# An FFN's transposed 32x32 squares by way of DRAM in place of SBUF-to-SBUF transfers

## The reference

```python
def _L0_ffn_ref(x, W1, b1, quantum_phases, quantum_weights_real, quantum_weights_imag, W2, b2):
    def _quantum_transform(hidden, theta, w_real, w_imag):
        imag = w_imag * jnp.sin(theta + hidden * 0.1)
        quantum_phase = jnp.cos(theta) * w_real + jnp.sin(theta) * w_imag
        return hidden + quantum_phase * imag * 0.1
    hidden = jnp.einsum('bsd,df->bsf', x, W1) + b1
    q = _quantum_transform(hidden, quantum_phases, quantum_weights_real, quantum_weights_imag)
    act = jax.nn.relu(q)
    return jnp.einsum('bsf,fd->bsd', act, W2) + b2
x = x + _L0_xattn_ref(_layernorm(x, axis=-1), ctx_768, ...)
x = x + _L0_ffn_ref(_layernorm(x, axis=-1), ...)
```

## Time and profile before

| | us |
|---|---|
| median of 3 runs | 2107.33 (2104.51 to 2107.42) |
| profiled execution | 2109.2 |
| its span, first to last instruction | 2107.4 |
| TensorE busy in the span | 2060.1 (98%) |
| VectorE, ScalarE, GpSimd busy | 1350.2, 1146.9, 1047.2 |
| mean granted TensorE clock | 0.995 |

### The profile page before, as it was taken

One profiled execution on the slowest core, in us unless ns is written; L12 is line 12 of the kernel. 1 busy time (PEld: TensorE's weight loads), 2 busy tenths in 40 slices (PEclk: granted clock), 3 DMA queues, 4 the chain that ended last, 5 costly groups with the idle time before them and its releaser, 6 DMA issues.

```text
span 2107.4 us, 27424 instructions
## 1 busy us (share of the span) xinstructions
PE 2060.1 (98%) x9746; PEld 1716.9 (81%) x9746; DVE 1350.2 (64%) x2024; ACT 1146.9 (54%) x2036; POOL 1047.2 (50%) x757
## 2 busy tenths in 40 slices
PE   7999999999999979999999999999999999999999
PEld 5888888888887868888888888888888888887877
DVE  5888898888876746555465554655556555465554
ACT  4766667667664645444554545545455444554543
POOL 3777777777775434353343533435334353343521
PEclk9999999999999989999999999999999999999999
DMA  5122232232213311101011010110101101011000
GB/s 180 56 93 93 81 101 97 84 101 80 75 56 121 99 31 44 58 17 44 21 43 58 17 44 21 42 59 17 44 20 43 58 18 44 21 44 58 14 27 20
DMA packets 123386, 118.25 MB, mean 56 GB/s; under 512 B 73961, under 2 KB 74473, under 8 KB 123249
## 3 DMA queue, kind: packets, MB, share of 16 engines
q1 hardware_dynamic: 122096, 115.93, 17.3%
q10 hardware_dynamic: 1152, 0.56, 0.1%
HBM read 66.10 MB, written 34.62 MB: 48 GB/s over the span
## 4 chain that ended last, share of the span: by engine, by line
PE 65%; SPq 13%; DVE 9%; ACT 4%; issue 4%; DMA 4%; POOL 1%; DVEq 0%; POOLq 0%; ACTq 0%
PE psum L1091 21%; PE psum L1093 20%; PE psum L1092 20%; SPq L431 13%; DMA xn<-stage 3%; PE psum L1172 2%; DVE hid L1024 2%; DVE xt_lo L1057 2%; PE psum L1097 1%; ACT act_hi L779 1%; DVE stage L1082 1%; DVE stage L1078 1%; DVE act_lo L1027 1%; ACT hid L790 1%; ACT frac L775 1%
## 5 line engine op out<-in xcount | busy, mean ns | idle before, releaser
L612 POOL TENSOR_TENSOR frac<-turns,frac 128x512 f32<-128x512 f32 x256 | 339.6, 1326 | 846.3 <-DVE frac L1052 846.3
L1091 PE MATMUL psum<-w_hi,act_hi 128*128 128x512 f32 x1024 | 401.6, 392 | 15.9 <-DVE act_lo L1027 15.9
L1024 DVE SCALAR_TENSOR_TENSOR hid<-frac,gain,hid 128x512 f32<-128x512 f32 x256 | 315.2, 1231 | 133.5 <-ACT frac L775 132.4
L1093 PE MATMUL psum<-w_hi,act_lo 128*128 128x512 f32 x1024 | 399.5, 390 | 0.0
L1092 PE MATMUL psum<-w_lo,act_hi 128*128 128x512 f32 x1024 | 399.4, 390 | 0.0
L779 ACT ACTIVATE act_hi<-hid 128x512 fp32r<-128x512 f32 x256 | 161.8, 632 | 366.1 <-DVE hid L1024 366.1
L788 ACT ACTIVATE turns<-psum,u_shift 128x512 f32<-128x512 f32 x256 | 176.5, 689 | 308.8 <-PE psum L1093 235.2
L1027 DVE SCALAR_TENSOR_TENSOR act_lo<-hid,act_hi 128x512 fp32r<-128x512 f32 x256 | 201.4, 787 | 178.8 <-ACT act_hi L779 178.8
L1052 DVE TENSOR_SCALAR frac<-turns 128x512 f32<-128x512 f32 x256 | 111.6, 436 | 221.5 <-ACT turns L788 221.4
L1091 PEld LDWEIGHTS psum<-w_hi,act_hi 128*128 128x128 f32 x1024 | 192.9, 188 | 63.5 <-DVE act_lo L1027 12.8
L1093 PEld LDWEIGHTS psum<-w_hi,act_lo 128*128 128x128 f32 x1024 | 192.8, 188 | 40.2
(11 more groups left out here) (147 smaller groups left out, 4179.4 us busy)
## 6 DMA issues: line engine op xcount, KB each, us to landing
res<-in_x SPq DMA_DIRECT2D x64, 256.0 KB, 2.9
x_dram<-res SPq DMA_DIRECT2D x64, 256.0 KB, 2.0
x_sb<-x_dram SPq DMA_DIRECT2D x16, 1024.0 KB, 5.5
x_sb<-in_x SPq DMA_DIRECT2D x15, 1024.0 KB, 5.9
xn<-stage SPq DMA_DIRECT2D x480, 32.0 KB, 1.9
out<-x_sb SPq DMA_DIRECT2D x15, 1024.0 KB, 4.5
stage<-in_w SPq DMA_DIRECT2D x32, 256.0 KB, 2.8
v_in<-v_dram SPq DMA_DIRECT2D x16, 128.0 KB, 3.0
```

The source lines that it names most:

```text
L612: pool.tensor_tensor(frac[:, j % 2, :], turns[:, j % 2, :], frac[:, j % 2, :], ALU.subtract)\
L1024: dve.scalar_tensor_tensor(out=hid[:, j % 2, :], in0=frac[:, j % 2, :], scalar=gain[:, f:f + 1], in1=hid[:, j % 2, :], op0=ALU.mult, op1=A ...
L1091: pe.matmul(o, a_hi, b_hi, start=first, stop=False)
L1093: return pe.matmul(o, a_lo, b_hi, start=False, stop=last)
```

## The change

The turned squares take another way. Per half SyncE writes `stage` to a DRAM buffer `turn_dram` in 4 transfers, one for each group a of 32 partitions, 4 KB a partition in four runs of 1 KB (128 KB a transfer), and later reads the half back into `xn` in one transfer of 128 partitions, 4 KB of contiguous DRAM a partition, put down in sixteen runs of 256 B (512 KB). A new semaphore pair `moved` counts the writes. VectorE's transposes wait for `moved`, where they waited for `turned_in`; ScalarE's copy waits for the reads. SyncE issues both halves' writes first, then waits for `moved[0]` and issues the first read, then the same for the second. Before the writes of a later tile it waits for the former reads (`turned_in`). The squares' order in `stage` and `xn` changes with it (`turned`, `channels`): VectorE's transposes write and ScalarE's and VectorE's copies read at other strides.

```diff
-TURNS = NB * NB
...
-        turn_done, turned_in = sem("turn_done"), sems("turned_in", 2)
+        turn_done, moved, turned_in = sem("turn_done"), sems("moved", 2), sems("turned_in", 2)
...
-        to_turn = xn[:].rearrange("p n c -> p (n c)").rearrange("p (q h x) -> p h q x", h=2, q=KC * NB)
-        turned = stage[:].rearrange("p s c -> p (s c)").rearrange("p (q x) -> p q x", q=KC * NB)
-        squares_out = stage[:].rearrange("p s c -> p (s c)").rearrange("p (k b x) -> p k b x", k=KC, b=NB)
-        squares_in = xn[:].rearrange("p n c -> p (n c)").rearrange("p (k a h x) -> p h k a x", k=KC, a=NB, h=2)
-        channels = xn[:].rearrange("p n c -> p (n c)").rearrange("p (k a n i) -> p k n a i", k=KC, a=NB, i=SQ)
+        to_turn = xn[:].rearrange("p n c -> p (n c)").rearrange("p (k b h x) -> p h k b x", k=KC, b=NB, h=2)
+        turned = stage[:].rearrange("p s c -> p (s c)").rearrange("p (b k x) -> p k b x", b=NB, k=KC)
+        squares_out = stage[:].rearrange("p s c -> p (s c)").rearrange("p (b y) -> p b y", b=NB)
+        squares_in = xn[:].rearrange("p n c -> p (n c)").rearrange("p (q h x) -> p h q x", q=KC * NB, h=2)
+        moved_out = turn_dram.rearrange("h b j a y -> h a j b y")
+        moved_in = turn_dram.rearrange("h b j a y -> h (b j) (a y)").rearrange("h p (q x) -> h p q x", q=KC * NB)
+        channels = xn[:].rearrange("p n c -> p (n c)").rearrange("p (a k n i) -> p k n a i", k=KC, a=NB, i=SQ)
...
                 for half in range(2):
                     sp.wait_ge(turn_done, 2 * t + half + 1)
+                    if t:
+                        sp.wait_ge(turned_in[half], 16 * t)
                     for a in range(NB):
-                        for b in range(NB):
-                            sp.dma_start(squares_in[b * SQ:(b + 1) * SQ, half, :, a, :],
-                                         squares_out[a * SQ:(a + 1) * SQ, :, b, :]).then_inc(turned_in[half], 16)
+                        sp.dma_start(moved_out[half, a], squares_out[a * SQ:(a + 1) * SQ]).then_inc(moved[half], 16)
+                for half in range(2):
+                    sp.wait_ge(moved[half], 16 * NB * (t + 1))
+                    sp.dma_start(squares_in[:, half], moved_in[half]).then_inc(turned_in[half], 16)
                 sp.wait_ge(y2_done, NB * (t + 1))
...
                     for half in range(2):
-                        act.wait_ge(turned_in[half], 16 * TURNS * (t + 1))
+                        act.wait_ge(turned_in[half], 16 * (t + 1))
...
                     if t:
-                        dve.wait_ge(turned_in[1], 16 * TURNS * t)
+                        dve.wait_ge(moved[1], 16 * NB * t)
...
                     dve.wait_ge(xn_done, TILES + t + 2)
-                    dve.wait_ge(turned_in[0], 16 * TURNS * (t + 1))
+                    dve.wait_ge(moved[0], 16 * NB * (t + 1))
...
+    turn_dram = nc.dram_tensor("turn_dram", (2, NB, P // NB, NB, 2 * C // NB), F32, kind="Internal").ap()
```

More of the change, by code:

```diff
@@ L112, in xattn_ffn @@
 def xattn_ffn(nc, x, ctx_768, wq, bq, wk, bk, wv, bv, wo, bo, w1, b1, phases, w_real, w_imag, w2, b2,
-              out, x1_dram, v_dram, u_dram):
+              out, x1_dram, v_dram, u_dram, turn_dram):
     x_rows = x.rearrange("b (t n p) c -> (b t) p n c", n=NB, p=P)
@@ L1351 @@
     u_dram = nc.dram_tensor("u_dram", (B, C), F32, kind="Internal").ap()
-    xattn_ffn(nc, *args, out, x1_dram, v_dram, u_dram)
+    turn_dram = nc.dram_tensor("turn_dram", (2, NB, P // NB, NB, 2 * C // NB), F32, kind="Internal").ap()
+    xattn_ffn(nc, *args, out, x1_dram, v_dram, u_dram, turn_dram)
     r = run_bass_kernel_spmd(nc, [arrays], core_ids=[0])
```

## The result

| | before | after |
|---|---|---|
| median, us | 2107.38 (4 runs, 2104.51 to 2109.45) | 2084.03 (4 runs, 2082.80 to 2084.35) |
| ratio | | 0.9889, 95% interval 0.9872 to 0.9906 |
| span of the profiled execution | 2107.4 | 2082.6 |
| TensorE busy | 2060.1 | 2051.2 |
| granted clock | 0.995 | 0.998 |

The change makes the kernel 1.1% faster; 2083.5 us had been forecast. In the changed file the lines are 5 further down: L1083 and L1087 are the transposes, L801 the copy to xt_hi, L1062 the one to xt_lo, L1032 act_lo; L434 is now a write, L437 a read.

The account below looks back on a forecast made before the run. TensorE's holes in the tile turns, from chains of 2 x 16 issues at 0.64 us, were taken as what can be won: 13.8 (turns) + 10.0 (tile 0) = 23.8 us off 2107.33 gives 2083.5 us; range 2079 to 2100, about 8 in 10.

Parts of the forecast that it names:

- What bounds: TensorE is busy 2060.1 of 2107.4 us; only its holes, in the turns between FFN tiles, can be won.
- Issues: SyncE, per half: 16 issues become 4 at 0.64 us; the fourth write goes out after 1.9 us, lands in 1.93 us.
- signs of being wrong: A half's pieces over 4.3 us, a read's issue holding SyncE for microseconds, or DRAM writes landing later than 2 us.
- Second transpose in the turns: VectorE, tiles 1 to 14: no wait for transfers, so it starts at 1113.16 instead of 1114.85.
- The reads: DRAM to xn: 3.3 us a half at 160 GB/s; second lands at 1125.5, at most 1126.5, leaving TensorE no hole.
- The rule of the Trainium skill: Small pieces from HBM cost more: a half's read 4.5 us, second landing near 1127.9, a hole of about 0.3 us left.
- The turns' 13.8 us: Tiles 1 to 14: 9.3 us of TensorE holes plus 4.5 us of surcharge at 0.28 us a hole go.
- Tile 0's 10.0 us: Tile 0's turn: second transpose 7.9 us earlier, copy to xt_hi 9.35 us earlier, next tile's product 10.0 us earlier.
- Access patterns: Transposes and copies to xt_hi and xt_lo at other strides, same elements and shapes: priced at nothing.
- The one with the slower reads: Rival: DRAM reads of 5.6 us a half make the turns lose more than tile 0 wins; 2132 us; 11%.
- 2T - 8.4: Cost in us of each turn's hole, surcharge included, when a half's read takes T; holes open from T = 4.3 us.

Follow-up runs that it names:

- b1: The changed kernel, but each half is read back as soon as its own writes are down; 2083.50 us (ratio 0.9882).
- b2: The changed kernel, but the reads put down 4 KB runs instead of sixteen of 256 B, squares in wrong places; 2082.58 us (one run).
- a2: The changed kernel, but only tile 0 goes by way of DRAM; tiles 1 to 14 use sixteen SBUF transfers per half; 2096.66 us (0.9942).
- a3: The changed kernel, but with sixteen writes of 32 KB per half in place of four of 128 KB; 2125.89 us (1.0079).
- a4: The kernel before, with only four of the sixteen SBUF transfers per half, the other squares left out; 2082.24 us (0.9881).
- c2: The changed kernel, but a 32 KB read must land before the second half's read is issued; 2088.07 us (0.9895).

## Why the prediction was right

The mechanism was right: issues made the chain, and the chain made the holes. That the time came out 0.5 us from the forecast is in part luck. In the profiled executions the two parts win 14.3 + 11.0 = 25.3 us and not 23.8, the changed kernel comes to the turn of tile 0 0.5 us later, and between the medians the difference is 23.4 us.

**What bounds.** Right. The holes of TensorE in the turns and in tile 0 were the whole of what could be won, and both parts came back, alone and together.

**Issues.** Right in kind; a write's issue is quicker than the 0.64 us step that was taken over: 0.44 us and 0.04 us between two. The landing was priced too low, 1.93 us; it is 2.4 us at the median and up to 4.1. Writes that land later than 2 us stood among the signs of being wrong; they did, and it did no harm, since the second transpose of a turn comes ten microseconds behind the first writes and the slack behind the reads took up the rest. The two errors cancel for the second transpose of tile 0: predicted 3.9 us behind the first write, measured 753.72 - 749.91 = 3.8.

**Second transpose in the turns.** Right: it waits for nothing; the only wait left is that of tile 0.

**The reads.** The second one was to land 12.3 us behind the start of the second transpose, at 1125.5 against 1113.16. Its issue was expected 5.1 us behind that start and came 1105.78 - 1099.27 = 6.5 us behind, and the read was down 10.9 us behind it, in the 14 turns 10.4 to 12.0. ScalarE came 1112.05 - 1099.27 = 12.8 us behind, as reckoned. Two mis-sized terms cancel here. The transfer time of a half is 1.8 to 2.0 us and not 3.3, which is the lower bound that the prediction gave. It took 160 GB/s from the old transfers because a burst of 0.35 us is mostly its ramp, and this reason is not borne out: the first writes of a half are also of 32 partitions and four times as long, and for a microsecond from 1090.2 us on the rate stays at 174 to 225 GB/s, not far above the burst's 148 to 169. The changed kernel, 1090 to 1094 us in slices of 0.1 us:

```profile
GB/s 0 72 195 174 195 205 184 184 174 225 215 195 154 143 164 226 318 379 379 338 307 236 205 174 174 31 0 0 0 0 0 0 0 0 0 0 0 0 0 0
```

A read of 128 partitions is faster, so the width of the old transfers may have held them down; no run separates it from the route and the size of the pieces.

In turn the second half's last write takes up to 4.1 us to land where 1.93 were taken. The read behind it is not the cause: in b1's turn above no read is under way from 1093.1 to 1101.2, and the write of 1097.50 still lands in 3.7 us. What goes with it is a 16 KB packet on the queue that the page calls instruction. In b1, window 1097.5 to 1101.3, and a later turn, 1794.4 to 1798.2, in which that queue has none:

```profile
q8 instruction: 1, 0.02, 1.7%
turn_dram<-stage SPq DMA_DIRECT2D x1, 128.0 KB, 3.7
...
turn_dram<-stage SPq DMA_DIRECT2D x1, 128.0 KB, 2.3
```

In b1 the last write of the second half lands in 3.02 to 3.85 us in the eight tiles with such a packet beside it and in 2.25 to 2.35 in the other seven, in the changed kernel in 2.72 to 4.05 (nine tiles) and 2.40 to 2.61 (six). No run takes the packets away. What the reads cost each other b1 does show: apart they land in 4.2 to 5.0 us, close together in 4.4 to 6.3. The prediction gave them a wait on SyncE but no share of each other's engines.

**The rule of the Trainium skill.** The section "Why small descriptors are slow (HBM only)" of DMA: Bandwidth & Descriptors in the Trainium skill gives 256 B pieces 11 cycles for 8, on an estimate 1.38 times the time. b2 against the changed kernel shows some 370 to 289 GB/s by the first read's plateau, 1.28 times, and 370 to 267 by the average of the second's, 1.39 times. The trace agrees with the rule in size. Where the prediction used it, it was laid on 3.3 us, which already was too long; on 1.4 us it leaves the read inside the slack.

**The turns' 13.8 us.** Measured from the product at 770.57 us (781.06 before) to the end: 1326.3 us before, 1312.0 after, 14.3 us, against 13.8. a2, with the old transfers in these turns and the changed kernel's layout, has 12.0 us; each of the three is one profiled execution.

**Tile 0's 10.0 us.** From the first transfer of the turn (749.39, now 749.91) to that product it is 31.67 us before and 20.66 after: 11.0 us. The hole for the second act_lo was predicted at 1.4 and is 1.2, the copy's start predicted 9.35 us earlier and is 10.4 (765.22 - 749.91 = 15.31 us behind the first transfer, 775.15 - 749.39 = 25.76 before). Of that microsecond 0.9 us is the issues of the writes: the first read was to be issued 757.2 - 749.4 = 7.8 us behind the first write and is issued 756.79 - 749.91 = 6.9 us behind. From there to the second read's landing it is 765.14 - 756.79 = 8.3 us where 8.5 were reckoned, since in tile 0 the faster transfer is nearly used up by the wait for the second half's writes, 2.2 us, and by two reads under way at once. The stretch at 0.50 of the earlier trace rows was not lost time: after it ScalarE's copy still waited 4.11 us for the transfers. The lower clock that cost something is the one behind the 3.12 us hole: twelve matmuls took 781.06 - 776.65 = 4.41 us before, 3.85 now with a wait of 0.85 among them.

**Access patterns.** Priced at nothing. The transposes take 1.24 and 1.23 us as before; the four copies to xt_hi 0.627 us against 0.617, xt_lo 0.680 against 0.686. Right.

**The rivals.** The one with the slower reads needed 4.9 us a half. a3 shows that its mechanism and price were sound, though there issues and not DRAM make the read late: it lands on average 16.4 us behind the start of the second transpose, where the changed kernel has 11.1, and the turns cost (1345.0 - 1312.0) / 14 = 2.4 us each. The rival's price 2T - 8.4 gives 2.3 for that landing (5.74 + 2T = 16.4).

## What to carry to other kernels

When many small transfers stand between two engines, count the issues on the queue first: here sixteen of 0.64 us are a chain of 10 us for 512 KB, and a detour through DRAM that moves twice the bytes is shorter, as it needs fewer of them. Then look for the slack of the engine that bounds the kernel, not of the one that waits: the copy here could be 1.57 us late before TensorE noticed, and that number, read from two turns, priced the change and three of the experiments.

## What the runs showed of the hardware that was not expected

- The issue of a DMA hardly grows with the pieces. From DRAM to 128 partitions 2048 pieces of 256 B take 0.53 us on SyncE and 128 of 4 KB 0.39 us (b2): sixteen times the pieces for 0.14 us more. With 32 partitions and 128 pieces it is 0.60 us from SBUF to SBUF (256 B each) and 0.43 us to DRAM (1 KB each).
- A plateau of 246 to 293 GB/s for 256 B pieces from DRAM to 128 partitions of SBUF, against 169 GB/s at the peak of a burst of 32 KB between 32 and 32 partitions: the one was no guide to the other.
- The last write of a second half, 128 KB, lands 0.7 to 1.6 us later in the tiles in which a 16 KB packet of the instruction queue is under way beside it (eight of eight in b1, none of the other seven).
- The start of tile 0's turn moves between executions of kernels that are alike up to there: the first transfer is issued at 746.38 (b1), 747.00 (a4), 749.91 (changed kernel), 751.21 us (a2). That spread of 4.8 us is larger than what b1 wins, and it is why the comparisons above go from the first transfer of the turn on. What in the attention part makes it was not looked for.
- The granted clock in tile 0. Before, it is 0.55 in 760 to 765 us, inside the 7.39 us hole, 0.50 in the earlier trace rows, back at 0.93 in 770 to 775, and 0.75 in 775 to 780, behind the 3.12 us hole. In c2 it is 0.81 and 0.50 during and behind a hole of 3.5 us. In the changed kernel, with no hole above 1.4 us there, every window from 740 to 790 us has 1.00. The rows of before:

```profile
760.00:765.00 5.00, 0.00 (x0) 0.00 (x0) 3.09 (x4) 0.63 (x1) 1.70 (x1) 0.55 0.10 23
...
775.00:780.00 5.00, 3.35 (x10) 2.68 (x11) 3.49 (x6) 3.34 (x6) 0.00 (x0) 0.75 0.00 0
```
